# A 12-column memset on GpSimd behind each gather of a GNN's edge stage

## The reference

```python
x  = x + gnn(layernorm(x), src, dst)
x  = x + ffn(layernorm(x))
# gnn:
neigh = segment_sum(node_feats[src], dst, num_segments=n)     # gather 200000 rows, add them by destination
h = (1 + eps) * node_feats + neigh
h = relu(h @ W1 + b1) @ W2 + b2                               # 256 -> 512 -> 256
h = (h - mean) * rsqrt(var + 1e-5) * gamma + beta             # statistics over the nodes
# ffn: softmax gate over 8 experts, top-1, capacity ceil(1.25 * T / 8) each,
#      relu(x @ w1[e] + b1[e]) @ w2[e] + b2[e] (256 -> 1024 -> 256), times the gate's probability
```

## Time and profile before

| what | us |
|---|---|
| median of 3 runs without the profiler | 2559.24 (2556.51 to 2567.18) |
| profiled execution, its span from first to last instruction | 3175.1 |
| GpSimd busy in the profiled execution | 1710.4, 1187.7 of it in the gathers |
| TensorE busy (matmuls) | 1826.2 |
| VectorE busy | 1442.5 |
| ScalarE busy | 694.9 |

### The profile page before, as it was taken

The page is one execution under the profiler, slowest core; times in us unless marked ns, Lnnn a source line. Parts: engine busy times, 40 slices in busy tenths (PEclk is TensorE's granted clock), DMA queues, the critical chain, the costliest instruction groups (busy, mean ns, idle before and its releaser), DMA issues. The chain is left out here.

```text
span 3175.1 us, 32785 instructions
## 1 busy us (share of the span) xinstructions
PE 1826.2 (58%) x9046; PEld 1097.7 (35%) x9047; DVE 1442.5 (45%) x4225; ACT 694.9 (22%) x1116; POOL 1710.4 (54%) x1690
## 2 busy tenths in 40 slices
PE   0154444455545455655554455564568768989995
PEld 0022212222222222322222222232357645566664
DVE  8765511543225422531252112122336557786885
ACT  6600000000010001000100001110046554636642
POOL 0366664655645565555644444445315556767874
PEclk9976667676767677777877777777776688999997
DMA  7533354324633354234423332212246432222220
GB/s 244 188 104 106 116 184 138 106 88 132 197 101 91 115 182 148 87 121 144 152 65 121 120 111 65 67 54 79 54 145 216 131 93 75 71 84 73 79 83 18
DMA packets 201521, 361.08 MB, mean 114 GB/s; under 512 B 62117, under 2 KB 125947, under 8 KB 201334
## 3 DMA queue, kind: packets, MB, share of 16 engines
q0 software_dynamic: 69152, 185.00, 19.3%
q1 hardware_dynamic: 130038, 172.60, 16.8%
q10 hardware_dynamic: 2144, 1.05, 0.1%
HBM read 291.08 MB, written 71.92 MB: 114 GB/s over the span
## 5 line engine op out<-in xcount | busy, mean ns | idle before, releaser
L791 POOL DMA_INDIRECT halves<-table,halves x1240 | 1187.7, 958 | 1011.5 <-issue 367.1
L879 PE MATMUL e_sums<-halves 128*128 128x256 f16 x1920 | 334.7, 346 | 392.8 <-issue 244.1
L1062 DVE SCALAR_TENSOR_TENSOR nodes<-e_sums,above,nodes 128x256 f32 (+1 forms) x161 | 77.3, 480 | 967.0 <-remote 437.4
L879 PEld LDWEIGHTS e_sums<-halves 128*128 128x128 f16 x1920 | 229.6, 122 | 508.3 <-issue 425.7
L936 PE MATMUL e_up<-e_hT,W1s 128*128 128x512 f32 (+1 forms) x400 | 229.8, 734 | 234.9 <-ACT e_hT L985 140.2
L985 ACT ACTIVATE e_hT<-e_up 128x1024 f32<-128x1024 f32 (+1 forms) x25 | 25.2, 1007 | 1524.0 <-remote 1185.3
L1720 POOL TENSOR_TENSOR x_midl<-x_midf,x_midh 128x512 f16<-128x512 f32 x200 | 298.7, 1517 | 104.9 <-ACT x_midh L1854 99.4
L917 PE MATMUL e_tally<-w1f,counts 128*128 128x512 f16 x490 | 165.5, 480 | 281.6 <-DMA w1f<-table 204.9
L1126 DVE TENSOR_TENSOR counts<-counts,e_tally 128x490 f32 x220 | 159.8, 726 | 267.8 <-PE e_tally L907 147.9
L1810 PE MATMUL x_down<-halves,x_midh 128*128 128x256 f16 x1472 | 249.4, 277 | 16.6 <-DVE x_yb L1947 15.0
L1786 PE MATMUL x_up<-x_xTh,halves 128*128 128x512 f16 (+1 forms) x800 | 233.6, 371 | 3.1 <-ACT x_midh L1854 3.1
(11 more groups left out here) (208 smaller groups left out, 2752.4 us busy)
## 6 DMA issues: line engine op xcount, KB each, us to landing
w1f<-table SPq DMA_DIRECT2D x120, 512.0 KB
halves<-table,halves POOLq DMA_INDIRECT x1240
slot_rows<-halves SPq DMA_DIRECT2D x64, 268.0 KB
x_row<-slot_rows SPq DMA_DIRECT2D x32, 536.0 KB, 7.4
table<-halves SPq DMA_DIRECT2D x25, 512.0 KB, 2.9
counts<-in_x SPq DMA_DIRECT2D x24, 512.0 KB, 4.5
r_xin<-in_x SPq DMA_DIRECT2D x24, 512.0 KB
out<-r_row SPq DMA_DIRECT2D x24, 512.0 KB
```

Of the source, the lines that this page charges most:

```text
L791: pool.indirect_dma_start(got[:, r, t, :], None, table.rearrange("p h d -> (p h) d"), bass.IndirectOffsetOnAxis(ap=idx[:, r, t:t + 1], axi ...
L879: ins = nc.tensor.matmul(sums[:, place, 0:D], hot[:, place, t, :], got[:, r, t, half * D:(half + 1) * D], start=(t == 0 and half == 0), st ...
```

## The change

A scratch `between` of 8 x 12 f32 columns and a semaphore `s_spaced` are added. `gather` issues, behind each indirect DMA, a GpSimd memset of 12 columns of that scratch (each of a group's eight has its own 12 columns). The memset raises `s_spaced` by one. Since the next group writes the same columns again, each group but the first begins with a wait until `s_spaced` counts all memsets of the groups before; in the loops the count is kept in a register.

```diff
+        between = sb("e_between", [P, 12 * GT], F32)
+        s_spaced = sem("e_spaced")
...
-                def gather(r):
+                def gather(r, spaced):
+                    if spaced is not None:
+                        pool.wait_ge(s_spaced, spaced)
+                        if not isinstance(spaced, int):
+                            pool.reg_add(spaced, spaced, GT)
                     for t in range(GT):
                         pool.indirect_dma_start(
                             got[:, r, t, :], None, table.rearrange("p h d -> (p h) d"),
                             bass.IndirectOffsetOnAxis(ap=idx[:, r, t:t + 1], axis=0)).then_inc(s_got[r], 16)
+                        nc.gpsimd.memset(between[:, t * 12:t * 12 + 12], 0.0).then_inc(s_spaced, 1)
 
                 for r in range(RG):
                     pool.wait_ge(s_idx[r], 16)
-                    gather(r)
+                    gather(r, r * GT if r > 0 else None)
+                spaced = counter(pool, "spaced", RG * GT)
...
-                        gather(r)
+                        gather(r, spaced)
...
-                    gather(r)
+                    gather(r, (NG - NG % RG + r) * GT)
```

## The result

The changed kernel takes 2660.0 us (median of 4 runs, 2656.1 to 2664.6), the kernel before 2562.7 us on the same chip (4 runs, 2556.5 to 2567.2). The ratio is 1.038, 95% interval 1.035 to 1.040: 97 us slower. The forecast was 2644 us.

A forecast was written before the change was run, and what follows sets the result against it. GpSimd's own queue, nearly full, was taken to bound the edge stage. Clears of 87 us plus head waits of 20 us gave 107, taken as 85 between two readings: 2559 + 85 = 2644 us, 8-in-10 range 2520 to 2715 us.

The forecast's parts named there:

- The clears: 1240 memsets, one behind each gather in GpSimd's queue, at 0.07 us each: 87 us of queue time.
- rival 1: Hidden: the 0.30 us between gathers has room for the memset, the head's wait is covered; 2559 us, chance 0.13.
- The wait at the head: Each group after the first waits for the memset directly ahead in GpSimd's queue: 0.12 to 0.13 us, 154 times, 20 us.
- the profile's reading: GpSimd's queue paces 75% of the first edge stretch, waits cover the second's added time: only 62 us added.
- What bounds the kernel: Edge stage in timed runs: most likely GpSimd's own queue, nearly full, one gather starting every 1.25 us, 1553 us in all.
- the sum 118 + 1553 + 885: Normalization, unhindered gathers, and routing with experts: 2556 us with no wait at all, against a median of 2559.
- the stop of the earlier trace: Around 262 to 272 us VectorE, TensorE and GpSimd stop, VectorE for 8.85 us; taken as largely the profiled execution's, no dependence.
- Rival 2's weaker form: Gathers lying further apart might shorten the stops of all engines, which end when the gathers pause.
- the 3237 us expected for the profile's kind of execution: Changed kernel's time in the profile's own terms: about 3175 + 62 us.
- rival 2: Faster: a memset between gathers shortens the gap by 0.05 to 0.11 us each; about 2500 us, chance 0.25.
- Rival 3: A full 0.30 us gap on both sides of each memset, 0.40 us per gather: 3050 us; 0.06, shared with VectorE's lock.
- VectorE's lock: Two-port VectorE operations could lock out the memsets in the edge stage: 45 us more, slow side only; 0.06 with Rival 3.

The follow-up runs named there:

- z1: Changed kernel with all 1240 memsets, but each head waits for those of three groups earlier; 2566.9 us against 2562.5 for the kernel before, ratio 1.002.
- x0: The kernel before, unchanged, profiled a second time on another chip: 3143.4 us; its unprofiled runs there have a median of 3146.7 us.
- y0: The changed kernel, unedited, on a chip where the kernel before takes 3118.6 us: 3069.7 us, ratio 0.985.
- x1: Changed kernel with all memsets, scratch for three groups, waiting for memsets three groups earlier; 3148.4 us, ratio 0.999 to the kernel before on a slow chip.
- w2: Changed kernel with memsets only behind each group's fourth and eighth gather, each waited for directly; 2964.2 us against 3156.7 for the kernel before, ratio 0.937.

## Why the prediction came out right, and what in it was wrong

The sign and the total were right: +85 us forecast, +97 measured. The split was not, and the total came out by luck: two errors of opposite sign.

**The clears** were the mis-sized term. I gave them 0.07 us each, 87 us of the 107. z1 measures them at +5 us in all (1.002); inside groups the median from start to start is 1.257 us there, against 1.252 in the kernel before. The 0.30 us between gathers absorbs a 0.125 us memset: 0.125 + 0.18 = 0.305. That is the mechanism of rival 1, which I had worked out correctly (0.05 + 0.10 + 0.15) and set aside because the profile shows "0.30 us without exception". The evidence for it was in the earlier trace rows, the 0.16 us behind a tensor_tensor, and I let it count for half. The marker that I had named gave the answer at once: 1.29 to 1.35 us would support the forecast, 1.25 rival 1, and it is 1.26.

**The wait at the head** was mis-sized the other way: 0.13 us from the earlier trace rows, 0.59 us measured, 20 us forecast and 91 us found. The row that I read was a scatter behind a 16x1 memset, which had another memset and no gather ahead of it; its 0.28 us idle stands against 0.77 here. That the gather ahead of the memset is the reason for the difference was not tested. The mark that I had named for the head, a gap of 0.4 us, is 0.89 us (706.75 - 705.86). The range would have needed a term of 154 x 0.59 and had none; I left the bound of a drain open on the high side.

The two errors happen to cancel nearly: 87 became 5, 20 became 91, together 107 and 96. I halfway discounted 107 to 85 for the profile's reading; the chip that decided had no cover for either term, so the full sum would have been the right one to take (2666 us).

**What bounds the kernel** was right for the chips that gave the median: the edge stage is GpSimd's own queue, and z1, 5 us above the kernel before, shows it: 1592 us of gathers against 1553 unhindered. Its waits there are small: of the 31.9 us for the index load 30.1 lie before the first gather, and TensorE's turn and the sums take 14.7 and 5.3. That the sum 118 + 1553 + 885 came within 3 us of the median is partly luck, for the 885 us are those of a chip of kind B: z1's own terms are 118 + 1592 + 854 = 2564 us. The prediction was wrong about why the profile differed. I took the stop of the earlier trace rows to belong to the profiled execution; x0 shows the same stop within half a microsecond of the same place, and unprofiled runs as slow. It belongs to the chip, and it was a dependence after all: VectorE waited for TensorE's late results, and GpSimd for VectorE's. With a profile from one kind of chip and a median from another, the arithmetic against the median was the part to trust, and the rows of waits were the part that could not be used for it.

**Rival 2's weaker form**, that gathers further apart shorten the stops, is what happens on chips of kind B (0.985 for the change, 0.937 with two drains), mostly by the drain rather than by the spacing. So the 3237 us expected for the profile's kind of execution had the wrong sign: y0 takes 3069.7 us, against 3118.6 for the kernel before. On a chip of kind A there is no stop to shorten. I had put rival 2 as a whole at 0.25 without asking on which execution's stops it rested. **Rival 3** is excluded by the 1.26 us.

**VectorE's lock.** About one memset in seven of the changed kernel takes over 0.15 us (168 of 1240, up to 0.69), but all that the memsets add is z1's 5 us, 9 us at the upper end of its interval, where I had worked out 45 from the rule. The lock rule of the Trainium skill (SBUF — State Buffer, Who interferes with whom) is thus not contradicted, but worth at most about 10 us here; it was not measured by itself. The rule of the Trainium skill (Perfetto Trace Analysis, GPSIMD Engine Instruction) to go by start-to-start spacing rather than by spans held: the 173.2 us busy that the profile gives the memsets stand for about 5 us of time.

No version beats both kernels on a chip of kind A: x1's wait three groups back only gives the change's cost back. On a chip of kind B w2 beats both.

## What to carry to other kernels

A small GpSimd operation between two indirect DMAs can be free, because the gap between them has room for it; a wait for an operation directly ahead in the same queue is not: it cost 0.59 us each time here. Look back by a few buffers and it costs nothing. When the profiled execution is far from the median, first run the same kernel again: a bottleneck read from the one may not exist in the other, and the same edit can have opposite signs on the two.

## What the runs showed of the hardware that I had not expected

- Two levels of one kernel by chip (or session), 2560 and 3120 to 3160 us, with TensorE's semaphore changes up to 20.9 us behind the modelled end of the matmul on kind B and 0.01 us on the other. The granted clock over 118 to 1600 us is 0.73 (x0) against 0.82 (z1), with TensorE less busy there.
- A pause of 0.59 us in the stream of gathers, twice a group, takes 6.3% off the run on such a chip.
- Two memsets of six columns behind a gather cost 0.01 us more than one of twelve: 1.27 against 1.26 us from gather to gather.
